# Two changes in a transformer kernel: row-maximum pieces in five of six attention steps, and a 64-row block padded to 128 rows

## The chip, the cores and the metric

The kernel runs on one core of a Trainium2 chip. A core has five engines that run side by side and wait for each other through semaphores: TensorE (PE in the profile: matmuls; PEld its weight loads), VectorE (DVE), ScalarE (ACT), GpSimd (POOL) and SyncE (SP, which issues transfers). Matmul results land in PSUM, eight banks of 512 columns; everything else stands in SBUF. The metric is the device time in microseconds (us) of one execution.

## The reference, cut to what matters

Two transformer layers over 2 x 1024 tokens of 256 features, each layer an attention and a feed-forward part, each followed by a sum with its input and a layer norm. The change touches the second layer alone: its softmax attention (16 heads, 128 plain and 64 rotated query columns, values of 128) and its feed-forward part with integer weights (704 hidden features).

```python
q = (x @ wq).reshape(b, s, H, QH).transpose(0, 2, 1, 3)
...
scores = jnp.einsum('bhqd,bhkd->bhqk', qs, ks_) * scale
scores = jnp.where(causal, scores, jnp.finfo(scores.dtype).min)
attn = jax.nn.softmax(scores, axis=-1)
out = jnp.einsum('bhqk,bhkd->bhqd', attn, v)
...
gate = jax.nn.silu(_qlinear(x, wq_gate, s_gate))
up = _qlinear(x, wq_up, s_up)
return _qlinear(gate * up, wq_down, s_down)
```

Batch and length come from the input, so there are two sequences of 1024 tokens; the attention is causal.

## The kernel before, in words

Float32 products are made from parts of shorter mantissa: a tile `x` is split into `x_hl[0]` (high) and `x_hl[1]` (the rest), and three matmuls (high-high, high-low, low-high) stand for one. So for each such tile ACT copies the high part, and POOL or DVE subtracts it to get the low part.

**Attention** (`phase_attention`, once per sequence, 16 heads). Keys are projected back into a shared space of 128 columns, so all heads use one `k_hl` and one `v_hl`; what is made per head is `q_hl`. Heads go in rounds of four (`rounds`, a hardware loop over rounds with its last one written out). A head has six steps x = 0 to 5, one for each group of two key tiles: groups 0 and 1 serve the first 512 queries, groups 2 to 5 the last 512. Every engine has a function `step(u, r, x, ...)` that lists what it does in that step, in its own program order, and waits for the others by counted semaphores. In step x of head r

- PE makes the scores two groups ahead (`scores`, L1386 products, L1390 mask, L1392 subtraction of the row maximum): in step 0 those of group 2, in steps 4 and 5 those of groups 0 and 1 of the next head. It also makes pieces of the next head's row maxima (`max_piece`, L1370, with L1373 for a piece on the diagonal), query tiles for the next pair of heads (`queries` L1348, `turn` L1362) and the values of group x (`values`, L1406).
- ACT takes the exponential (`probs` L1465), copies the high part (`highs` L1472), copies queries (`row` L1452, `q_high` L1458) and, after groups 1 and 5, the sums (`sums` L1480, L1481).
- POOL subtracts for the low part of the probabilities (`low` L1525) and adds the two halves of the rotation (`rotated` L1519).
- DVE reduces each maximum piece (`peaks` L1578), multiplies for the rotation (`rope` L1561, L1564), makes the queries' low part (`q_low` L1572), and divides the sums of an earlier head (`divide`, L1605 reciprocal and L1607 product). When all pieces of a half are in, `spread` joins them (L1587, or L1590 for the first half) into `whole` and writes `minus` (L1593), a diagonal tile with the negated maxima, which `scores` of the next head need: the first half's in step 4, the second half's (group 2) in step 0 of the next head.

A head's maxima come in twelve pieces, numbered 0 to 11. Row tiles 0 to 3 have one piece (128, 256, 384 and 512 columns wide), row tiles 4 to 7 have two (384 and 256, 512 and 256, 512 and 384, 512 and 512 columns), the second of which lies on the diagonal. The list that sets which piece stands in which step is

```python
PIECES_AT = [(0, 1, 2), (3, 4), (5, 6), (7, 8), (9, 10), (11,)]
```

The first piece of a step stands between the two halves of the scores, a middle one after them, and the last one between the two halves of the values. Two PSUM banks take the pieces in turn, so piece y waits until piece y - 2 is reduced. In heads with even r query tiles are made in all six steps, in heads with odd r only in steps 4 and 5; DVE divides in steps 0 to 3 of heads with even r and in steps 2 to 5 of heads with odd r. In step 1 of odd r DVE also splits new query weights (`weights`).

**Feed-forward part** (`phase_feed_forward`). Tokens go in 4 chunks of 512, hidden features in 6 blocks: five of 128 and a last one of 64 (`HT`). For each chunk and block PE makes gate and up products (`gate_up`, L1889), ACT the activation (L1933) and the high part (L1924), DVE the product of the two (L1973), POOL the low part (L1947). `down_of(t)` (L1902) makes the output of one tile of 128 tokens: 2 parts times 6 blocks, twelve matmuls of 256 columns, of which the two of the last block have 64 rows. The four tiles of a chunk stand between the gate and up products of the next chunk; those of the last chunk stand at the end. The phase begins behind a barrier of all engines.

Of the kernel before, what the change touches and what calls it, by code (L numbers as in the profile page):

```python
# [13 lines left out]
F32 = mybir.dt.float32  # L14
# [8 lines left out]
P = 128  # L23
B, S, C = 2, 1024, 256
# [32 lines left out]
HT = [(n * P, min(P, HID - n * P)) for n in range((HID + P - 1) // P)]  # L57
# [1158 lines left out]
def phase_attention(nc, name, bank, cst, bf, x_hl, wqk_rows, w_raw, w_hl, k_hl, v_hl, oT, last_den):  # L1216
# [10 lines left out]
    with Memory(nc, name) as m:  # L1227
# [38 lines left out]
        AHEAD = 2  # L1266
        HEADS = 4
        ROUNDS = H // HEADS
        PIECES_AT = [(0, 1, 2), (3, 4), (5, 6), (7, 8), (9, 10), (11,)]
        QUARTERS = WIDE // P  # L1270

        def span(group):
# [49 lines left out]
        with nc.Block() as block:  # L1322
# [224 lines left out]
            def _(dve):  # L1547
# [61 lines left out]
                def step(u, r, x, more, peak_pieces, made, turned):  # L1609
                    for y in peak_pieces[:1]:  # L1610
                        peaks(u, r + 1, y)
                    if made:
                        rope(u, *made)
                    for y in peak_pieces[2:]:
                        peaks(u, r + 1, y - 1)
                    if more and x == NG - 1:
                        spread(u, r + 1, 1)
                    if turned:
                        q_low(u, *turned)
                    for y in peak_pieces[1:][-1:]:  # L1620
                        peaks(u, r + 1, y)
                    if more and x == 1:
                        spread(u, r + 1, 0)
                    if r % 2 and x == 1 and not is_round(u, ROUNDS - 1):
                        weights(u, r // 2 + 2)
                    if r % 2 and x >= 2:
                        divide(u, r // 2, 0, x - 2)
                    if r % 2 == 0 and x < QUARTERS and not (is_round(u, 0) and r == 0):
                        divide(u, r // 2 - 1, 1, x)
# [218 lines left out]
def phase_feed_forward(nc, bank, x_hl, x_tok, power, quantised, out):  # L1848
# [4 lines left out]
    NHT = len(HT)  # L1853
    with Memory(nc, "ffn") as m:
# [6 lines left out]
        z = x_tok  # L1861
        norm = LayerNorm(nc, m, z, x_tok, power, 0, NT, 2)
        stored = m.sem("stored")
        gu_mm, gate_sb, hid_sb, hi_sb, lo_sb, y_mm, scaled_sb, z_sb = (
            m.sem(n) for n in ("gu_mm", "gate_sb", "hid_sb", "hi_sb", "lo_sb", "y_mm", "scaled_sb", "z_sb"))
        CT = WIDE // P
# [3 lines left out]
        with nc.Block() as block:  # L1870
            @block.sync
            def _(sp):
                for g in range(norm.groups):
                    sp.wait_ge(norm.x_sb, 2 * (g + 1))
                    at = slice(2 * g, 2 * (g + 1))
                    sp.dma_start(out.rearrange("(t p) c -> p t c", p=P)[:, at, :], x_tok[:, at, :]).then_inc(stored, 16)
                sp.wait_ge(stored, 16 * norm.groups)

            @block.tensor
            def _(pe):  # L1880
                def gate_up(ch, n):
                    h0, hw = HT[n]
                    x = ch * NHT + n
                    if x >= 2:
                        pe.wait_ge(hid_sb, x - 1)
                    for a in range(2):
                        for i in range(2 * KC):
                            part, k = divmod(i, KC)
                            mm = nc.tensor.matmul(bank[0:hw, 2 * (x % 2) + a, :], w[:, a, k, h0:h0 + hw],  # L1889
                                                  x_hl[:, part, k, ch * WIDE:(ch + 1) * WIDE],  # L1890
                                                  start=i == 0, stop=i == 2 * KC - 1)
                    mm.then_inc(gu_mm, 1)

                def down_of(t):
                    ch, i = divmod(t, CT)
                    if t >= 4:
                        pe.wait_ge(z_sb, t - 3)
                    for part in range(2):
                        for n, (h0, hw) in enumerate(HT):
                            if t % CT == 0:  # L1900
                                pe.wait_ge(lo_sb if part else hi_sb, ch * NHT + n + 1)
                            mm = nc.tensor.matmul(bank[:, 4 + t % 4, 0:C], hid_hl[0:hw, part, ch % 2, n, i * P:(i + 1) * P],  # L1902
                                                  down[0:hw, n, :], start=part == 0 and n == 0,
                                                  stop=part == 1 and n == NHT - 1)
                    mm.then_inc(y_mm, 1)

                pe.wait_ge(quantised.w_sb, 4)
                for ch in range(NCH):
                    for n in range(NHT):
                        gate_up(ch, n)  # L1910
                        if ch and 0 <= n - FIRST_DOWN < CT:
                            down_of((ch - 1) * CT + n - FIRST_DOWN)
                for t in range(NT - CT, NT):
                    down_of(t)

            @block.scalar
            def _(act):
                def high(x):
                    n, ch = x % NHT, x // NHT
                    hw = HT[n][1]  # L1920
                    act.wait_ge(hid_sb, x + 1)
                    if n == 0 and ch >= 2:
                        act.wait_ge(y_mm, (ch - 1) * CT)
                    nc.scalar.copy(hid_hl[0:hw, 0, ch % 2, n, :], hid[0:hw, x % 2, :]).then_inc(hi_sb, 1)  # L1924

                act.wait_ge(scales, 16 * (2 * NHT + 1))
                for x in range(NCH * NHT):
                    n = x % NHT
                    hw = HT[n][1]
                    act.wait_ge(gu_mm, x + 1)  # L1930
                    if x >= 2:
                        act.wait_ge(hid_sb, x - 1)
                    nc.scalar.activation(gate[0:hw, x % 2, :], bank[0:hw, 2 * (x % 2), :], ACT.Silu,  # L1933
                                         scale=s_gate[0:hw, n:n + 1]).then_inc(gate_sb, 1)
                    if x:
                        high(x - 1)
                high(NCH * NHT - 1)

            @block.gpsimd
            def _(pool):  # L1940
                for x in range(NCH * NHT):
                    n, ch = x % NHT, x // NHT
                    hw = HT[n][1]
                    if x in norm_at:
                        norm.deviations(pool, norm_at[x])
                    pool.wait_ge(hi_sb, x + 1)
                    nc.gpsimd.tensor_tensor(hid_hl[0:hw, 1, ch % 2, n, :], hid[0:hw, x % 2, :],  # L1947
                                            hid_hl[0:hw, 0, ch % 2, n, :].bitcast(F32), ALU.subtract).then_inc(lo_sb, 1)
                for g in range((NT - CT) // 2 - 1, NT // 2):
                    norm.deviations(pool, g)  # L1950

            @block.vector
            def _(dve):
                def sum_of(t):
                    dve.wait_ge(y_mm, t + 1)
                    nc.vector.tensor_tensor(scaled[:, t % 2, :], bank[:, 4 + t % 4, 0:C], s_down[:],  # L1956
                                            ALU.mult).then_inc(scaled_sb, 1)
                    dve.wait_ge(scaled_sb, t + 1)
                    nc.vector.tensor_tensor(z[:, t, :], scaled[:, t % 2, :], x_tok[:, t, :], ALU.add).then_inc(z_sb, 1)  # L1959
                    if t % 2:  # L1960
                        if t >= 2:
                            norm.normalise(dve, t // 2 - 1)
                        dve.wait_ge(z_sb, t + 1)
                        norm.statistics(dve, t // 2)

                dve.wait_ge(scales, 16 * (2 * NHT + 1))
                for ch in range(NCH):
                    for n, (h0, hw) in enumerate(HT):
                        x = ch * NHT + n
                        dve.wait_ge(gate_sb, x + 1)  # L1970
                        if x >= 2:
                            dve.wait_ge(lo_sb, x - 1)
                        nc.vector.scalar_tensor_tensor(hid[0:hw, x % 2, :], bank[0:hw, 2 * (x % 2) + 1, :],  # L1973
                                                       s_up[0:hw, n:n + 1], gate[0:hw, x % 2, :], ALU.mult,
                                                       ALU.mult).then_inc(hid_sb, 1)
                        if ch and 0 <= n - FIRST_DOWN < CT:
                            sum_of((ch - 1) * CT + n - FIRST_DOWN)
                for t in range(NT - CT, NT):
                    sum_of(t)
                norm.normalise(dve, NT // 2 - 1)  # L1980
# [92 lines left out]
```

## Time and profile before

| | us |
|---|---|
| median of 3 runs | 1520.33 |
| lowest and highest run | 1519.51, 1523.01 |
| the profiled execution | 1521.97 |
| its span, first to last instruction | 1519.4 |
| PE busy | 1295.9 (85%) |
| DVE busy | 966.3 (64%) |
| POOL busy | 821.3 (54%) |
| ACT busy | 653.8 (43%) |

The attention of the two sequences lies at about 500 to 930 and 975 to 1390 us of the span, the feed-forward part from 1429 us on. A row of the timeline has the start, the duration, engine, line, operation, what it writes and reads, shape and count; a bracket at its end is the idle time of its engine just before it and what ended it. A row of the waits says which engine and line waited for which, how long in total, how often, and the longest. A row of the groups by form has the count, the busy time in us, the mean in ns of one, and the idle time before them. A row of the critical chain has the start, the time and the line with its count. Idle time counts where the engine is the one that the others wait for.

### The profile page before, as it was taken

The page shows a single profiled execution, that of the slowest core. Times are in us where ns is not written, and L with a number is a line of the kernel's source. Part 1 is how long each engine was busy: PE and PEld are TensorE (multiplying, and loading weights), DVE is VectorE, ACT ScalarE, POOL GpSimd, SP SyncE. Part 2 cuts the span into 40 slices and gives each one's busy share as a digit, 9 for nine tenths or more (in the row PEclk, how much of TensorE's full clock was granted, in tenths as well). Part 3 has the DMA queues.
Part 4 walks back from the last instruction along what each step waited for, and adds up shares of the span by engine and source line. Part 5 has one row for each costly group of instructions (what it writes and reads, how often), then busy time and mean ns, then how long its engine had stood idle before and what let it go on. Part 6 is the DMA issues. An engine that isn't in the chain of part 4 may idle for free. (4 is left out here: it accounts for less than half of the span.)

```text
span 1519.4 us, 23881 instructions
## 1 busy us (share of the span) xinstructions
PE 1295.9 (85%) x7096; PEld 976.6 (64%) x7097; DVE 966.3 (64%) x2055; ACT 653.8 (43%) x1183; POOL 821.3 (54%) x652
## 2 busy tenths in 40 slices
PE   6965799999944899998999987799999999888797
PEld 5854455555523677776776767677676777767675
DVE  4568422222217778877687768768777877875555
ACT  3211233333212555555555553265555555555332
POOL 2016688888845455545455556354555555556444
PEclk9976799999985999999999999999999999999899
DMA  9357255555552000000000000000000000002001
GB/s 326 121 167 175 86 83 80 80 82 80 80 107 67 8 8 8 1 7 7 1 7 0 2 0 12 15 1 8 8 7 0 7 7 0 1 1 62 1 14 42
DMA packets 66218, 67.13 MB, mean 44 GB/s; under 512 B 15040, under 2 KB 59648, under 8 KB 66016
## 3 DMA queue, kind: packets, MB, share of 16 engines
q1 hardware_dynamic: 48048, 42.38, 9.5%
q0 software_dynamic: 15168, 20.72, 8.8%
q10 hardware_dynamic: 2928, 3.15, 0.7%
q8 instruction: 35, 0.57, 0.2%
q14 instruction: 39, 0.32, 0.1%
HBM read 45.12 MB, written 21.10 MB: 44 GB/s over the span
## 5 line engine op out<-in xcount | busy, mean ns | idle before, releaser
L1525 POOL TENSOR_TENSOR att_prob_lo<-att_prob,att_prob_hi 128x896 fp32r<-128x896 f32 (+1 forms) x192 | 380.4, 1981 | 223.4 <-ACT att_prob_hi L1472 223.4
L1386 PE MATMUL all_bank<-att_q_hl,sequence_k_hl 128*128 128x512 f32 (+2 forms) x1152 | 289.4, 361 | 43.2 <-DVE att_minus L1593 43.0
L1578 DVE TENSOR_REDUCE att_peak<-all_bank 128x1 f32<-128x512 f32 (+3 forms) x384 | 207.8, 550 | 95.0 <-PE all_bank L1373 61.2
L1406 PE MATMUL all_bank<-att_prob_hi,sequence_v_hl 128*128 128x512 f32 (+2 forms) x768 | 225.1, 376 | 12.1 <-ACT late_oT L1481 12.1
L1386 PEld LDWEIGHTS all_bank<-att_q_hl,sequence_k_hl 128*128 128x128 f32 x1152 | 191.6, 192 | 63.9 <-DVE att_minus L1593 33.3
L1465 ACT ACTIVATE att_prob<-all_bank 128x896 f32<-128x896 f32 (+1 forms) x192 | 162.8, 848 | 157.8 <-PE all_bank L1392 156.4
L1370 PE MATMUL all_bank<-sequence_k_hl,att_q_hl 128*128 128x512 f32 (+3 forms) x384 | 164.7, 432 | 6.8 <-DVE att_peak L1578 6.8
L1472 ACT CAST att_prob_hi<-att_prob 128x896 fp32r<-128x896 f32 (+1 forms) x192 | 168.4, 877 | 2.6
L1519 POOL TENSOR_TENSOR att_rows<-att_by_cos,att_by_sin 128x128 f32<-128x128 f32 x128 | 58.5, 457 | 198.6 <-DVE att_by_sin L1564 198.6
L903 PE MATMUL all_bank<-early_w_gu,moe_xgT 128*128 x316 | 147.2, 548 | 3.6 <-issue 2.4
L1406 PEld LDWEIGHTS all_bank<-att_prob_hi,sequence_v_hl 128*128 128x128 f32 x768 | 128.5, 191 | 27.0 <-issue 16.6
L868 POOL DMA_INDIRECT sums<-moe_y,early_slot_far x79 | 125.4, 1587 | 33.9 <-issue 18.9
L1452 ACT COPY att_rows<-all_bank 128x256 f32<-128x256 f32 x128 | 47.5, 371 | 219.9 <-PE all_bank L1348 219.9
L1348 PE MATMUL all_bank<-sequence_w_hl,sequence_x_hl 128*128 128x256 f32 x768 | 125.9, 301 | 15.5 <-DVEq L1633 8.0
L1406 PE MATMUL all_bank<-att_prob_lo,sequence_v_hl 128*128 128x512 f32 (+2 forms) x384 | 133.2, 347 | 0.0
L1392 PE MATMUL all_bank<-att_minus,all_bf 128*128 128x512 bf16 (+2 forms) x384 | 131.5, 342 | 0.0
L1348 PEld LDWEIGHTS all_bank<-sequence_w_hl,sequence_x_hl 128*128 128x128 f32 x768 | 103.6, 197 | 18.0 <-issue 8.8
L995 DVE COPY moe_hidT<-all_bank 112x256 f32<-112x256 f32 x79 | 33.5, 424 | 121.8 <-PE all_bank L913 121.8
L1607 DVE TENSOR_TENSOR late_oT<-late_oT,att_rden 128x128 f32 (+1 forms) x120 | 91.2, 760 | 11.4 <-DVE att_rden L1605 1.6
L858 POOL DMA_INDIRECT moe_xg<-x_rows,early_slot_row x79 | 84.0, 1063 | 26.1 <-issue 21.5
L922 PE MATMUL all_bank<-early_w_down,moe_hidT 112*128 x316 | 86.7, 397 | 13.1 <-issue 11.3
L1370 PEld LDWEIGHTS all_bank<-sequence_k_hl,att_q_hl 128*128 128x128 f32 x384 | 74.3, 194 | 16.7 <-DVE att_peak L1578 8.1
(244 smaller groups left out, 2299.7 us busy)
## 6 DMA issues: line engine op xcount, KB each, us to landing
sequence_w_raw<-wqk_rows SPq DMA_DIRECT2D x16, 256.0 KB, 2.7
early_w_gu<-in_gate SPq DMA_DIRECT2D x16, 224.0 KB, 5.4
early_w_gu<-in_up SPq DMA_DIRECT2D x16, 224.0 KB, 5.5
early_w_down<-in_down SPq DMA_DIRECT2D x1, 3584.0 KB, 20.5
sums<-early_zero SPq DMA_DIRECT2D x18, 128.0 KB, 3.6
all_xT<-in_xT SPq DMA_DIRECT2D x4, 512.0 KB, 8.7
all_x_tok<-in_x SPq DMA_DIRECT2D x1, 2048.0 KB, 17.1
x_rows<-all_x_tok SPq DMA_DIRECT2D x4, 512.0 KB, 3.0
```

Of the source, the lines that this page charges most:

```text
L868: nc.gpsimd.indirect_dma_start(sums[s], bass.IndirectOffsetOnAxis(slot_far[:, r:r + 1], 0), y[:, s, :], None, bounds_check=last_far, compu ...
L903: mm = nc.tensor.matmul(gu_ps[s], xgT[:, s, k, :], w_gu[:, bass.ds(e * (KC * 2 * I) + k * 2 * I, 2 * I)], start=k == 0, stop=k == KC - 1)
L1348: mm = nc.tensor.matmul(q_bank(u, r, t), x_hl[:, xs, k, t * P:(t + 1) * P], w_hl[:, ws, k, :], start=n == 0, stop=n == 3 * KC - 1)
L1370: mm = nc.tensor.matmul(ps[:, 0:w], q_hl[r // 2 % 2][:, 0, r % 2, i * P:(i + 1) * P], k_hl[:, 0, k0:k0 + w], start=True, stop=not diagonal)
L1386: nc.tensor.matmul(ps, k_hl[:, ks, j * P:(j + 1) * P], q_hl[r // 2 % 2][:, qs, r % 2, q0:q0 + w], start=n == 0, stop=False)
L1392: mm = nc.tensor.matmul(ps, bf["ones"], minus[:, r % 2].rearrange("p i m -> p (i m)")[:, q0:q0 + w], start=False, stop=True)
L1406: mm = nc.tensor.matmul(pv_ps[:, q0 - qc * WIDE:WIDE], v_hl[:, vs, j, :], part[:, x % 3, a:z], start=j == 0 and n == 0, stop=last and n == 2)
L1465: nc.scalar.activation(prob[:, x % 2, a:z], s_ps[x % 2][:, a:z], ACT.Exp, scale=SCALE).then_inc(prob_sb, 1)
L1472: nc.scalar.copy(prob_hi[:, x % 3, a:z], prob[:, x % 2, a:z]).then_inc(hi_sb, 1)
L1525: nc.gpsimd.tensor_tensor(prob_lo[:, x % 3, a:z], prob[:, x % 2, a:z], prob_hi[:, x % 3, a:z].bitcast(F32), ALU.subtract).then_inc(lo_sb, 1)
L1578: nc.vector.tensor_reduce(peak[:, r % 2, n, i:i + 1], max_ps[y % 2][:, 0:w], AX_X, ALU.max).then_inc(peak_sb, 1)
L1607: nc.vector.tensor_tensor(own, own, rden[:, n % 2, :], ALU.mult).then_inc(o_sb, 1)
```

## The change

The list of pieces is drawn forward by one piece per step from step 1 on, so that step 5 has none. The second `spread` of a head moves from step 5 to the end of step 4, behind the last maximum. In the feed-forward part the matmuls of the last block use all 128 rows of `hid_hl` and `down`. The 64 rows that nothing else writes are filled with zeros by POOL at the start of the phase, and PE waits for both fills before its first matmul there.

```diff
--- before.py
+++ after.py
@@ -1266,7 +1266,7 @@
         AHEAD = 2
         HEADS = 4
         ROUNDS = H // HEADS
-        PIECES_AT = [(0, 1, 2), (3, 4), (5, 6), (7, 8), (9, 10), (11,)]
+        PIECES_AT = [(0, 1, 2), (3, 4, 5), (6, 7), (8, 9), (10, 11), ()]
         QUARTERS = WIDE // P
 
         def span(group):
@@ -1613,12 +1613,12 @@
                         rope(u, *made)
                     for y in peak_pieces[2:]:
                         peaks(u, r + 1, y - 1)
-                    if more and x == NG - 1:
-                        spread(u, r + 1, 1)
                     if turned:
                         q_low(u, *turned)
                     for y in peak_pieces[1:][-1:]:
                         peaks(u, r + 1, y)
+                    if more and x == NG - 2:
+                        spread(u, r + 1, 1)
                     if more and x == 1:
                         spread(u, r + 1, 0)
                     if r % 2 and x == 1 and not is_round(u, ROUNDS - 1):
@@ -1861,6 +1861,7 @@
         z = x_tok
         norm = LayerNorm(nc, m, z, x_tok, power, 0, NT, 2)
         stored = m.sem("stored")
+        pad_sb = m.sem("pad_sb")
         gu_mm, gate_sb, hid_sb, hi_sb, lo_sb, y_mm, scaled_sb, z_sb = (
             m.sem(n) for n in ("gu_mm", "gate_sb", "hid_sb", "hi_sb", "lo_sb", "y_mm", "scaled_sb", "z_sb"))
         CT = WIDE // P
@@ -1899,12 +1900,13 @@
                         for n, (h0, hw) in enumerate(HT):
                             if t % CT == 0:
                                 pe.wait_ge(lo_sb if part else hi_sb, ch * NHT + n + 1)
-                            mm = nc.tensor.matmul(bank[:, 4 + t % 4, 0:C], hid_hl[0:hw, part, ch % 2, n, i * P:(i + 1) * P],
-                                                  down[0:hw, n, :], start=part == 0 and n == 0,
+                            mm = nc.tensor.matmul(bank[:, 4 + t % 4, 0:C], hid_hl[:, part, ch % 2, n, i * P:(i + 1) * P],
+                                                  down[:, n, :], start=part == 0 and n == 0,
                                                   stop=part == 1 and n == NHT - 1)
                     mm.then_inc(y_mm, 1)
 
                 pe.wait_ge(quantised.w_sb, 4)
+                pe.wait_ge(pad_sb, 2)
                 for ch in range(NCH):
                     for n in range(NHT):
                         gate_up(ch, n)
@@ -1938,6 +1940,9 @@
 
             @block.gpsimd
             def _(pool):
+                last = HT[NHT - 1][1]
+                nc.gpsimd.memset(hid_hl[last:P, :, :, NHT - 1, :].bitcast(F32), 0.0).then_inc(pad_sb, 1)
+                nc.gpsimd.memset(down[last:P, NHT - 1, :].bitcast(F32), 0.0).then_inc(pad_sb, 1)
                 for x in range(NCH * NHT):
                     n, ch = x % NHT, x // NHT
                     hw = HT[n][1]
```

What this does to the order on DVE, at the end of a head with odd r in the loop (steps 4 and 5 up to the first query work of step 5; `att_peak` is a maximum piece, `att_whole` and `att_minus` are the spread, `att_rden` and `late_oT` the division, `by_cos` and `by_sin` the rotation). Before:

```order
L1578 TENSOR_REDUCE att_peak<-all_bank 128x1
L1605 RECIPROCAL att_rden<-att_den 128x128
L1607 ISA
L1607 TENSOR_TENSOR late_oT<-late_oT,att_rden 128x128
L1283 REGISTER_ALU
L1578 TENSOR_REDUCE att_peak<-all_bank 128x1
L1286 REGISTER_ALU
L1561 TENSOR_TENSOR att_by_cos<-att_rows,all_cst 128x128
L1564 TENSOR_TENSOR att_by_sin<-att_rows,all_cst 128x2x32 x2
L1587 TENSOR_TENSOR att_whole<-att_peak 128x4
L1283 REGISTER_ALU
L1593 SCALAR_TENSOR_TENSOR att_minus<-all_bf,att_whole 128x512
```

And of the change, from the same point:

```order
L1578 TENSOR_REDUCE att_peak<-all_bank 128x1
L1587 TENSOR_TENSOR att_whole<-att_peak 128x4
L1283 REGISTER_ALU
L1593 SCALAR_TENSOR_TENSOR att_minus<-all_bf,att_whole 128x512
L1605 RECIPROCAL att_rden<-att_den 128x128
L1607 ISA
L1607 TENSOR_TENSOR late_oT<-late_oT,att_rden 128x128
L1286 REGISTER_ALU
L1561 TENSOR_TENSOR att_by_cos<-att_rows,all_cst 128x128
L1564 TENSOR_TENSOR att_by_sin<-att_rows,all_cst 128x2x32 x2
L1572 TENSOR_TENSOR att_q_hl<-all_bank,att_q_hl 128x2x128
```

The spread now stands ahead of the division of step 4 and of step 5's rotation, and the piece of step 5 is gone.

On PE at the same place, step 4 from the second half of the scores on and the start of step 5 (`att_prob` are values, `att_q_hl,sequence_k_hl` scores, `sequence_k_hl,att_q_hl` of a maximum piece, `att_minus` the end of a half of the scores). Before:

```order
L1386 MATMUL all_bank<-att_q_hl,sequence_k_hl 128x384 x3
L1390 MATMUL all_bank<-all_bf 128x128
L1392 MATMUL all_bank<-att_minus,all_bf 128x384
L1406 MATMUL all_bank<-att_prob_hi,sequence_v_hl 128x512 x2
L1406 MATMUL all_bank<-att_prob_lo,sequence_v_hl 128x512
L1283 REGISTER_ALU
L1370 MATMUL all_bank<-sequence_k_hl,att_q_hl 128x512
L1406 MATMUL all_bank<-att_prob_hi,sequence_v_hl 128x384 x2
L1406 MATMUL all_bank<-att_prob_lo,sequence_v_hl 128x384
L1283 REGISTER_ALU
L1386 MATMUL all_bank<-att_q_hl,sequence_k_hl 128x256 x3
```

And of the change:

```order
L1386 MATMUL all_bank<-att_q_hl,sequence_k_hl 128x384 x3
L1390 MATMUL all_bank<-all_bf 128x128
L1392 MATMUL all_bank<-att_minus,all_bf 128x384
L1406 MATMUL all_bank<-att_prob_hi,sequence_v_hl 128x512 x2
L1406 MATMUL all_bank<-att_prob_lo,sequence_v_hl 128x512
L1283 REGISTER_ALU
L1370 MATMUL all_bank<-sequence_k_hl,att_q_hl 128x512
L1373 MATMUL all_bank<-all_bf 128x128
L1406 MATMUL all_bank<-att_prob_hi,sequence_v_hl 128x384 x2
L1406 MATMUL all_bank<-att_prob_lo,sequence_v_hl 128x384
L1283 REGISTER_ALU
L1386 MATMUL all_bank<-att_q_hl,sequence_k_hl 128x256 x3
```

The piece between the two halves of the values is now one on the diagonal, with a matmul of its mask behind it; the piece that followed in step 5 has moved here.

On POOL at the start of the feed-forward part, of the change (`ffn_hid_hl` the hidden values, `late_w_down` the down weights):

```order
L109 ISA
L1941 UNCONDITIONAL_BRANCH
L1944 MEMSET ffn_hid_hl 64x4x512
L1945 MEMSET late_w_down 64x256
L1952 TENSOR_TENSOR ffn_hid_hl<-ffn_hid,ffn_hid_hl 128x512 x5
L1952 TENSOR_TENSOR ffn_hid_hl<-ffn_hid,ffn_hid_hl 64x512
```

The two fills are new and stand ahead of the first subtraction; the rest is as before.

## Rows read from the trace of the kernel before

**Rows 1.** Waits of PE, both attention phases: line, releaser, us in total, times, longest.

```profile
PE all_bank L1386 <- DVE att_minus L1593: 43.0, 30, 2.8
...
PE all_bank L1370 <- DVE att_peak L1578: 6.8, 12, 0.6
```

**Rows 2.** Timeline of PE over two heads: start us, us, engine line op.

```profile
617.16 0.96 PE L1386 MATMUL all_bank<-att_q_hl,sequence_k_hl 128*128 128x512 f32 x3 [1.79 <-DVE att_minus L1593]
...
618.26 0.23 PE L1373 MATMUL all_bank<-all_bf 128*128 128x128 bf16 x1
618.30 0.96 PE L1348 MATMUL all_bank<-sequence_w_hl,sequence_x_hl 128*128 128x256 f32 x6
...
645.01 0.96 PE L1386 MATMUL all_bank<-att_q_hl,sequence_k_hl 128*128 128x512 f32 x3 [0.91 <-DVE att_minus L1593]
...
669.06 0.96 PE L1386 MATMUL all_bank<-att_q_hl,sequence_k_hl 128*128 128x512 f32 x3 [1.79 <-DVE att_minus L1593]
```

**Rows 3.** Timeline of DVE at the end of the second of these heads.

```profile
663.56 0.69 DVE L1578 TENSOR_REDUCE att_peak<-all_bank 128x1 f32<-128x512 f32 x1 [0.72 <-PE all_bank L1370]
...
665.25 1.60 DVE L1607 TENSOR_TENSOR late_oT<-late_oT,att_rden 128x128 f32 x1
666.78 0.68 DVE L1578 TENSOR_REDUCE att_peak<-all_bank 128x1 f32<-128x512 f32 x1
...
667.85 0.15 DVE L1587 TENSOR_TENSOR att_whole<-att_peak 128x4 f32<-128x4 f32 x1
668.03 0.97 DVE L1593 SCALAR_TENSOR_TENSOR att_minus<-all_bf,att_whole 128x512 bf16<-128x512 bf16 x1
668.92 0.41 DVE L1572 TENSOR_TENSOR att_q_hl<-all_bank,att_q_hl 128x256 fp32r<-128x256 f32 x1
```

**Rows 4.** Timelines of POOL and DVE, the first spread in step 1 of both heads.

```profile
627.48 2.38 POOL L1525 TENSOR_TENSOR att_prob_lo<-att_prob,att_prob_hi 128x1024 fp32r<-128x1024 f32 x1 [0.73 <-ACT att_prob_hi L1472]
...
627.59 2.82 DVE L1593 SCALAR_TENSOR_TENSOR att_minus<-all_bf,att_whole 128x512 bf16<-128x512 bf16 x1
...
652.79 0.69 DVE L1593 SCALAR_TENSOR_TENSOR att_minus<-all_bf,att_whole 128x512 bf16<-128x512 bf16 x1
```

**Rows 5.** Timelines of PE, ACT and POOL in step 4 of the second head.

```profile
663.13 0.39 PE L1370 MATMUL all_bank<-sequence_k_hl,att_q_hl 128*128 128x512 f32 x1
663.36 0.51 PE L1406 MATMUL all_bank<-att_prob_hi,sequence_v_hl 128*128 128x384 f32 x2
...
663.58 0.94 ACT L1472 CAST att_prob_hi<-att_prob 128x896 fp32r<-128x896 f32 x1
...
664.59 2.11 POOL L1525 TENSOR_TENSOR att_prob_lo<-att_prob,att_prob_hi 128x896 fp32r<-128x896 f32 x1 [1.22 <-ACT att_prob_hi L1472]
```

**Rows 6.** Timelines of DVE and POOL in step 4 of the first head.

```profile
640.81 0.68 DVE L1578 TENSOR_REDUCE att_peak<-all_bank 128x1 f32<-128x512 f32 x1
...
641.35 2.10 POOL L1525 TENSOR_TENSOR att_prob_lo<-att_prob,att_prob_hi 128x896 fp32r<-128x896 f32 x1 [1.35 <-ACT att_prob_hi L1472]
```

**Rows 7.** Timeline of PE; windows: busy of PE, PEld, DVE, ACT, POOL, then PEclk.

```profile
720.86 0.96 PE L1386 MATMUL all_bank<-att_q_hl,sequence_k_hl 128*128 128x512 f32 x3 [1.79 <-DVE att_minus L1593]
...
722.05:725.46 3.41, 3.41 (x15) 2.48 (x14) 0.47 (x2) 0.39 (x2) 0.00 (x0) 0.50 0.01 2
```

**Rows 8.** Critical chain of one tile; groups by form; timeline of the output projection.

```profile
1460.81 1.98 PE all_bank L1902 x12
...
L1902 PE MATMUL all_bank<-late_w_down,ffn_hid_hl 64*128 64x256 f32 x32 | 12.2, 381 | 0.2 <-POOL ffn_hid_hl L1947 0.2
...
1394.73 18.20 PE L1711 MATMUL all_bank<-all_vo,out_o_hl 128*128 128x256 f32 x152
```

**Rows 9.** Critical chain: start of the feed-forward part, and its last down products.

```profile
1429.02 3.48 PE all_bank L1889 x8
...
1504.37 6.99 PE all_bank L1902 x37
```

**Rows 10.** Groups by form: a fill on POOL elsewhere in the kernel.

```profile
L648 POOL MEMSET all_xT<- 128x2048 f32 x1 | 1.8, 1804 | 8.3 <-POOLq L110 8.3
```

## The prediction

> **What bounds the kernel now.** I read the waits of TensorE (PE) over both attention phases first. One wait leads: scores wait for the row maxima that VectorE (DVE) spreads into `minus`, 43.0 us in 30 times, and the next one that DVE causes is 6.8 us [rows 1]. The timeline of PE shows where it stands: at every change of head, before the scores of group 2. The head that starts at 617.16 ends in a wait of 0.91 us, the one from 645.01 in one of 1.79 us [rows 2], and this alternates through both phases. I call heads that end in 0.91 even (they also make the next pair's queries) and the others odd; the 30 waits are 16 even and 14 odd ones, and their average, 43.0 / 30 = 1.43 us, lies between. Third, the timeline of DVE at an odd head's end shows why: the last maximum (666.78), `whole` (667.85) and `minus` (668.03, 0.97 us) come at the very end, behind a product of 1.60 us at 665.25 [rows 3]. So in attention PE is the bound, and between heads it hangs on a chain of DVE.
>
> **The lock between DVE and GpSimd.** `minus` takes 0.69 us alone at 652.79, but 2.82 us at 627.59, where GpSimd's subtraction had started 0.11 us before it, at 627.48 for 2.38 us; it ended 0.55 us after GpSimd [rows 4]. So a `minus` that comes just behind a subtraction ends with it + 0.55 us. This decides what the move is worth, since the new place of `minus` is where GpSimd starts the next head's first subtraction. The Trainium skill (SBUF — State Buffer, "Who interferes with whom") says that a DVE instruction with two SBUF inputs contends with a GpSimd instruction that reads SBUF and that the first to start holds the pair for its whole length; the rows above agree, and by the rule too the winner of each race is what counts.
>
> **The move of the maxima.** No instruction is added: twelve pieces, two spreads, as before. One piece goes from step 5 to steps 1 to 4, and the second spread from step 5 to the end of step 4, ahead of the last division of that step.
> - Odd head. PE issues the piece of step 4 between the two value halves at 663.13, and the next matmul follows 0.23 us later [rows 5]. The piece there becomes the diagonal one, whose short matmul takes 0.23 us [rows 2]: its result stands at 663.13 + 0.23 + 0.23 + 0.04 = 663.63. The maximum takes 0.69 us as at 663.56, `whole` to `minus` 0.18 us [rows 3], with 0.04 us between: `minus` starts at about 663.63 + 0.69 + 0.04 + 0.18 = 664.54. ScalarE's copy ends at 663.58 + 0.94, and GpSimd's subtraction starts at 664.59 [rows 5]. Both chains hang on the same PE step, so the lead of 0.05 us stays when the head shifts. I take it that DVE is first: `minus` ends at 665.2, 2 us before PE is ready (669.06 - 1.79 = 667.27), and the 1.79 us go. The bound on the other side: GpSimd first, `minus` ends at 664.59 + 2.11 + 0.55 = 667.25, still in time, but rope and `q_low`, which stand behind it, stay where they are (`q_low` ends at 668.92 + 0.41 = 669.33 [rows 3]), while PE now comes to the queries 618.30 - 617.16 = 1.14 us after its start [rows 2], at 668.4. That is a new wait of 0.9 to 1.0 us, and only 0.8 us of 1.79 are left.
> - Even head. In step 4 DVE is held by `q_low` until its maximum at 640.81, while GpSimd's subtraction starts at 641.35 for 2.10 us [rows 6]. The maximum ends at 641.5, so `whole` and `minus` come after the subtraction's start: they end at 641.35 + 2.10 + about 0.75 = 644.2, and later by some 0.3 us, since in step 2 the wide piece now stands first and makes DVE late. PE is ready at 645.01 - 0.91 = 644.10. I keep 0.46 us of the 0.91, between 0.15 and 0.9.
> - Sum: 43.0 less 14 times 0.46 = 36.6 us (the even head at the end of each sequence makes no queries and has no `q_low` to be held by). The third piece in step 1 I cost at nothing: the spread behind it is held until GpSimd ends at 627.48 + 2.38 anyway [rows 4]. Without that cover it is one maximum of 0.42 us in each even head, 6 us in all.
>
> **The clock.** After the 1.79 us wait at 720.86 TensorE runs a stretch of 3.41 us at 0.50, that is 1.2 instead of 2.4 GHz [rows 7]. Five such stretches start within 2 us of a wait of this kind or of the 2.8 us one near 879; none starts behind a wait of 0.9 us. At most each costs 3.41 / 2 = 1.7 us, 8.5 us in all, and at least nothing comes back. I take 6.
>
> **The padded block.** Twelve down matmuls of one tile take 1.98 us on the critical chain [rows 8]. The 152 matmuls of the same 128x256 shape in the output projection, all with 128 rows, take 18.20 us, 0.120 us each or 1.44 for twelve [rows 8]. The two 64-row ones of a tile are what differs: their mean is 381 ns [rows 8]. With 128 rows I expect the spacing of the others, 0.54 us per tile, 8.6 us over 16 tiles. At the end tile 12 stands before GpSimd's last `lo` (PE goes on at 1504.37 [rows 9]), so what tile 11 and half of tile 12 gain is waited away: 1.5 tiles, 0.8 us. Left 7.8; the bounds are 0 and 8.6.
> The Trainium skill (TensorE: Matmul & The Clock Gate, "Why this matters for your kernels") has a matmul over 32 rows take the same time as one over 128. By that the padding buys nothing; the 381 ns speak against it here, and it is a rival below.
> Against it stand two fills on GpSimd, which PE now waits for. A fill of 2048 columns took 1.80 us [rows 10]; the other, of 256, is 0.23 at that rate. GpSimd and PE leave the same barrier, and PE's first gate matmul starts at 1429.02 [rows 9], so its start moves by about 2.1 us. Nothing hides this, as the first activation hangs on that matmul; at most another 1.7 us of low clock comes with it, at least nothing if GpSimd leaves the barrier early. Net 7.8 - 2.1 = 5.7 us.
>
> **Sum.** 36.6 + 6 + 5.7 = 48.3 us off the profiled execution, whose own time is 1521.97 us (span 1519.4). That is 1.6 us above the median 1520.33. Against the median: 1520.3 - 48.3 = 1472.
>
> **The rivals.**
> - GpSimd wins the race in odd heads. For it: a lead of 0.05 us is less than what a register instruction more could eat. Against it: both chains are rigid. The 14 odd boundaries keep 1.0 us each, and some low clock stays: 14 + 2 less gain, 1488.
> - The waits come back elsewhere on DVE: the 6.8 us for maxima [rows 1] grow, as three pieces stand in step 1 and DVE is late in step 2 and 3. If each head loses 1 us more in this way, 30 us of the attention's gain are lost: about 1502.
> - The padded matmuls take what the 64-row ones take. Then only the fills are left: 7.8 us more, 1480.
> - Slower: the spread in step 4 is locked in every head, and the division behind it too, before rope and `q_low`. The place is the queries in step 0. The price is a lock of 2.1 + 0.55 us, and it decides from a mean of 1.43 + (6 + 5.7) / 30 = 1.8 us of new wait per head. At the full 2.65 us it gives 30 x (2.65 - 1.43) = 37 us more, less 5.7, with no clock back: about 1551. Against it: DVE has waits of its own in step 0 in which it catches up.
>
> **How the numbers follow.** Forecast (DVE first in odd heads) 0.50; GpSimd first 0.24; waits elsewhere 0.12; padding without gain 0.07, on top of either of the first two; slower 0.04; 0.03 for a sum near zero. The forecast's own range is 1462 to 1482: all 8.5 us of clock, 0.9 us in even heads and a free start below, 4 us of clock and 0.15 us in even heads above. The range for 8 in 10 takes in GpSimd first with its own spread: 1461 to 1496. About 0.2%, 3 us, is what a measurement of this kernel can tell from no change: faster 0.93, within 0.03, slower 0.04.
>
> **What would show it.** Right: the wait of scores for `minus` falls from 43.0 us to under 10; in odd heads `minus` starts just before the subtraction and takes 0.69 us; a tile's twelve down matmuls take 1.4 us; the gate matmuls start 2 us later after the barrier. Wrong: a `minus` of 2.6 us in odd heads with queries waiting for `q_low` about 1 us (the first rival); waits for maxima above 20 us (the second); down matmuls still at 1.98 us per tile (the third); queries waiting over 2 us in every head (the last).

## The result, and the profile after

The changed kernel takes 1470.3 us in the median of 4 runs (1462.73 to 1471.49), against 1520.56 (1519.51 to 1523.01) before: a ratio of 0.9656 with an interval of 0.9628 to 0.9683. The forecast was 1472, with a range of 1461 to 1496. The profiled execution took 1471.49 us. The ratios and intervals leave out runs that took more than 1.5% longer than the fastest of the same kernel: one of before (1534.59 us), and one of `later_spread` below, which took 3768.65 us for a cause that stays open.

```profile
span 1469.1 us, 23884 instructions
PE 1278.5 (87%) x7096; PEld 966.7 (66%) x7097; DVE 973.3 (66%) x2055; ACT 655.6 (45%) x1183; POOL 826.6 (56%) x654
```

It is best compared in three parts. The first, from the start to the first head of the attention, is touched by no edit, and yet lay between 503.9 and 517.9 us in the runs of this study. So the other two tell more than the totals. The first head starts where PE makes the scores of group 2 for it. The times are from the PE timeline and the critical chain of each profiled execution.

| us | to the first head | from it to the feed-forward part | feed-forward part |
|---|---|---|---|
| before | 514.3 | 914.6 | 90.5 |
| changed | 515.9 | 870.3 | 82.9 |
| difference | +1.6 | -44.3 | -7.6 |

The waits of PE in both attention phases of the changed kernel answer to [rows 1]; four of them tell the story:

```profile
PE all_bank L1370 <- DVE att_peak L1578: 10.9, 16, 1.6
PE all_bank L1406 <- ACT late_oT L1481: 7.4, 16, 1.1
...
PE all_bank L1348 <- DVE att_q_hl L1572: 6.0, 20, 0.4
PE all_bank L1386 <- DVE att_minus L1593: 5.7, 14, 0.5
```

The last was 43.0 us and the first 6.8 [rows 1]. The other two were, before:

```profile
PE all_bank L1406 <- ACT late_oT L1481: 12.1, 18, 1.1
...
PE all_bank L1348 <- DVE att_q_hl L1572: 5.5, 13, 0.4
```

Together 37.4 us of waiting are gone. The timeline of PE shows where, as [rows 2] did for before:

```profile
590.92 0.96 PE L1386 MATMUL all_bank<-att_q_hl,sequence_k_hl 128*128 128x512 f32 x3 [0.38 <-DVE att_minus L1593]
612.93 0.84 PE L1386 MATMUL all_bank<-att_q_hl,sequence_k_hl 128*128 128x512 f32 x3
...
628.41 0.50 PE L1370 MATMUL all_bank<-sequence_k_hl,att_q_hl 128*128 128x512 f32 x1 [0.66 <-DVE att_peak L1578]
629.31 0.95 PE L1348 MATMUL all_bank<-sequence_w_hl,sequence_x_hl 128*128 128x256 f32 x6 [0.39 <-DVE att_q_hl L1572]
```

The odd head from 590.92 to 612.93 takes 22.0 us, against 669.06 - 645.01 = 24.05 before, and ends in no wait. The even head behind it takes 27.66 us, against 27.85 before [rows 2]. Its wait at the end fell from 0.91 to 0.38 us (at 640.59, where the next odd head begins). Inside it stand waits of 0.66 and 0.39 us; the head of before had two much like them:

```profile
632.11 0.38 PE L1370 MATMUL all_bank<-sequence_k_hl,att_q_hl 128*128 128x256 f32 x1 [0.58 <-DVE att_peak L1578]
633.00 0.95 PE L1348 MATMUL all_bank<-sequence_w_hl,sequence_x_hl 128*128 128x256 f32 x6 [0.44 <-DVE att_q_hl L1572]
```

A wait of 0.17 us for `q_low` at 614.29 is new; waits of 0.16 to 0.25 us stand behind eleven of the odd heads in this way.

The ends of an odd and of an even head on DVE and POOL, which answer to [rows 3, 5] and [rows 6]:

```profile
609.69 0.69 DVE L1578 TENSOR_REDUCE att_peak<-all_bank 128x1 f32<-128x512 f32 x1 [0.79 <-PE all_bank L1373]
610.42 0.16 DVE L1587 TENSOR_TENSOR att_whole<-att_peak 128x4 f32<-128x4 f32 x1
610.62 0.69 DVE L1593 SCALAR_TENSOR_TENSOR att_minus<-all_bf,att_whole 128x512 bf16<-128x512 bf16 x1
...
610.67 2.61 POOL L1525 TENSOR_TENSOR att_prob_lo<-att_prob,att_prob_hi 128x896 fp32r<-128x896 f32 x1 [1.23 <-ACT att_prob_hi L1472]
...
637.13 0.68 DVE L1578 TENSOR_REDUCE att_peak<-all_bank 128x1 f32<-128x512 f32 x1
637.85 1.96 DVE L1587 TENSOR_TENSOR att_whole<-att_peak 128x4 f32<-128x4 f32 x1
639.84 0.69 DVE L1593 SCALAR_TENSOR_TENSOR att_minus<-all_bf,att_whole 128x512 bf16<-128x512 bf16 x1
...
637.68 2.11 POOL L1525 TENSOR_TENSOR att_prob_lo<-att_prob,att_prob_hi 128x896 fp32r<-128x896 f32 x1 [1.33 <-ACT att_prob_hi L1472]
```

In the odd head `minus` is first by 0.05 us, and it is POOL that is held (2.61 us where 2.11 is its own time). In the even head POOL is first by 0.17 us, and the tiny `whole` of 4 columns takes 1.96 us instead of 0.16. No half-clock stretch stands behind a change of head any more; there were five of 3.41 us before [rows 7]. (One stands at the start of the first head, from 514.52 to 517.93 us, where before had none.)

The critical chain at the start of the feed-forward part, where [rows 8, 9] stood:

```profile
1386.19 1.80 POOL ffn_hid_hl L1944
1387.99 0.26 POOL late_w_down L1945
...
1388.39 3.64 PE all_bank L1890 x8
...
1408.31 1.41 PE all_bank L1903 x12
1409.73 1.84 PE all_bank L1890 x8
```

The fills hold PE for 1388.39 - 1386.19 = 2.2 us. A tile's down products take 1.41 us instead of 1.98 [rows 8], and the eight gate products behind them 1.84 instead of 2.04, which the chain showed before:

```profile
1450.77 2.04 PE all_bank L1889 x8
```

### The profile page after: what moved, and what is told of

Its sections match the earlier page's. It is cut to its first block and busy times, and to the rows that moved or that the text cites. A ratio compares the mean times of both kernels' runs of the same rounds, so it can differ in the third digit from the quotient of the medians.

```text
span 1469.1 us, 23884 instructions
## 1 busy us (share of the span) xinstructions
PE 1278.5 (87%) x7096; PEld 966.7 (66%) x7097; DVE 973.3 (66%) x2055; ACT 655.6 (45%) x1183; POOL 826.6 (56%) x654
## 5 line engine op out<-in xcount | busy, mean ns | idle before, releaser
L1386 PE MATMUL all_bank<-att_q_hl,sequence_k_hl 128*128 128x512 f32 (+2 forms) x1152 | 282.5, 354 | 5.8 <-DVE att_minus L1593 5.7
L1406 PE MATMUL all_bank<-att_prob_hi,sequence_v_hl 128*128 128x512 f32 (+2 forms) x768 | 231.1, 384 | 7.5 <-ACT late_oT L1481 7.4
L1370 PE MATMUL all_bank<-sequence_k_hl,att_q_hl 128*128 128x512 f32 (+3 forms) x384 | 168.3, 441 | 11.1 <-DVE att_peak L1578 10.9
L1348 PE MATMUL all_bank<-sequence_w_hl,sequence_x_hl 128*128 128x256 f32 x768 | 121.9, 296 | 16.4 <-DVEq L1633 7.9
L1406 PEld LDWEIGHTS all_bank<-att_prob_hi,sequence_v_hl 128*128 128x128 f32 x768 | 120.3, 193 | 14.6 <-issue 12.0
L1607 DVE TENSOR_TENSOR late_oT<-late_oT,att_rden 128x128 f32 (+1 forms) x120 | 94.3, 786 | 11.4 <-DVE att_rden L1605 1.6
L922 PE MATMUL all_bank<-early_w_down,moe_hidT 112*128 x316 | 87.3, 399 | 12.6 <-issue 10.9
```

The source lines that it names most:

```text
L1348: mm = nc.tensor.matmul(q_bank(u, r, t), x_hl[:, xs, k, t * P:(t + 1) * P], w_hl[:, ws, k, :], start=n == 0, stop=n == 3 * KC - 1)
L1370: mm = nc.tensor.matmul(ps[:, 0:w], q_hl[r // 2 % 2][:, 0, r % 2, i * P:(i + 1) * P], k_hl[:, 0, k0:k0 + w], start=True, stop=not diagonal)
L1386: nc.tensor.matmul(ps, k_hl[:, ks, j * P:(j + 1) * P], q_hl[r // 2 % 2][:, qs, r % 2, q0:q0 + w], start=n == 0, stop=False)
L1406: mm = nc.tensor.matmul(pv_ps[:, q0 - qc * WIDE:WIDE], v_hl[:, vs, j, :], part[:, x % 3, a:z], start=j == 0 and n == 0, stop=last and n == 2)
L1607: nc.vector.tensor_tensor(own, own, rden[:, n % 2, :], ALU.mult).then_inc(o_sb, 1)
```

## The experiments

My theory: the odd heads gain because `minus` beats GpSimd's subtraction in step 4 by a hair; the even heads lose that race and keep some 0.4 us; the padding and the fills are worth what the chain shows, apart from the attention. The rival: it is drawing the pieces forward that matters, and the race decides nothing. Times in the text are medians against a before of 1520.3 to 1521.6 us; windows are the second and third column of the table.

**Each change alone.** `maxima_only` has the new list and the moved spread, `pad_only` only the feed-forward edits.

> The attention part of the change alone, the feed-forward part as before. From the two traces the feed-forward phase, barrier to end, takes 90.5 us before and 82.9 us after, so this kernel is expected 7.6 us above the changed one: 1478 us. The scores' wait for the maxima stays at 5.7 us. Rival: the two parts help each other (a PE that runs without gaps keeps its clock into the feed-forward part); then it is over 1483 us.

> The padded block alone, the attention as before: 1520.5 less 7.6, 1513 us, with the twelve down matmuls of a tile at 1.41 us and the wait of 43.0 us for the maxima unchanged. The rival that padding gains nothing by itself gives 1522.5 us (the fills alone, 2.1 us).

Measured: 1478.6 us (0.9696, 0.9597 to 0.9794) and 1514.1 (0.9937, 0.9896 to 0.9978). The second total is within 2% of before; the windows separate the two cleanly: 868.5 and 90.7 us for the first, 911.7 and 83.0 for the second. Within 3 us the two add up and don't act on each other. The attention of `pad_only` is that of before (42.9 us of waiting for `minus`), and its window is 2.9 us shorter: in that execution half-clock stretches stand behind three changes of head and not five (at 619.7, 879.1 and 1196.5 us, the second twice as long).

**The pieces drawn forward, the spread left in step 5** (`spread_stays`):

```diff
+                    if more and x == NG - 1:
+                        spread(u, r + 1, 1)
                     if turned:
                         q_low(u, *turned)
...
-                    if more and x == NG - 2:
-                        spread(u, r + 1, 1)
```

> The changed kernel with the pieces drawn forward, but the second spread left in step 5 behind the rotation. If what counts is where the spread stands (and which engine holds the port there), an odd head's spread comes behind the locked product of the division and the rotation, about 0.6 us earlier than in the kernel before, one maximum; the wait for the maxima stays above 20 us and the time is about 1498 us. Rival: the freed piece in step 5 is what gives the time; then the wait is under 10 us and the time 1470 to 1476 us.

```profile
PE all_bank L1386 <- DVE att_minus L1593: 39.7, 28, 2.9
```

Measured: 1505.0 us (0.9862, 0.9763 to 0.9961), window 903.9. The total is within 2% of before; again the window tells. The pieces alone take 3.3 us off the wait (39.7 against 43.0 us); 33.6 of the 44.3 us come from the spread's place. The other 10.7 us come with the list. Beside the 3.3 us, the waits on the sums' copy and on `q_low` fell by 4.7 and 2.4 us and those for maxima rose by 2.5. And with gaps at the heads' ends of 1.15 and 1.46 us instead of 0.91 and 1.79, four of the five half-clock stretches went (one is left, at 876.1 us). How the 10.7 us divide between waits and clock stays open.

**Whose turn it is in step 4.** `late_spread` puts a copy of 128 columns on DVE ahead of the second spread in odd heads, `later_spread` a reduction of 384 columns.

```diff
                     if more and x == NG - 2:
+                        if r % 2:
+                            nc.vector.tensor_reduce(spare[:], cst["cos"][:, 0:384], AX_X, ALU.max)
                         spread(u, r + 1, 1)
```

> The changed kernel with one more copy of 128 columns on DVE ahead of the second spread in heads with odd r: some 0.2 us of work, 3 us in all. If the 0.05 us by which the spread starts ahead of GpSimd's subtraction decides, GpSimd now starts first: minus takes about 2.6 us there, queries wait about 0.9 us for the late q_low, and 14 heads lose 0.8 to 1.2 us each: 1482 to 1487 us. Rival: DVE has the slack and the race decides nothing; then 1470 to 1473 us.

Measured: 1467.2 us, window 868.5. The copy fell into the time in which the spread waits for the maximum to end, and `minus` still came 0.04 us ahead of POOL (552.09 against 552.13). It did not move what it was to move, and tells nothing about the race.

> The changed kernel with one more DVE reduction of 384 columns from SBUF (about 0.47 us) between the last maximum and the second spread in heads with odd r; its result is used by nobody. The copy of 128 columns did not move the spread, since it ran in the time in which the spread waits for the maximum's end anyway; this one ends about 0.35 us later than that. If the race with GpSimd decides, GpSimd starts first: whole and minus end 0.6 to 0.75 us behind it, queries wait about 1 us for q_low, and odd heads go from 22.05 to between 22.8 and 23.3 us; the attention of both sequences is 10 to 17 us longer. Rival: DVE has the slack; the odd heads stay within 0.1 us of 22.05.

Measured: 1483.8 us (0.975, 0.9729 to 0.9771), window 892.0, 21.7 more than the change (by the medians, in which the uneven first part lies too, it is 13.5). An odd head's end on DVE, POOL and PE:

```profile
609.50 0.54 DVE L1623 TENSOR_REDUCE att_spare<-all_cst 128x1 f32<-128x384 f32 x1
609.96 2.05 DVE L1588 TENSOR_TENSOR att_whole<-att_peak 128x4 f32<-128x4 f32 x1
612.04 0.69 DVE L1594 SCALAR_TENSOR_TENSOR att_minus<-all_bf,att_whole 128x512 bf16<-128x512 bf16 x1
...
609.87 2.12 POOL L1526 TENSOR_TENSOR att_prob_lo<-att_prob,att_prob_hi 128x896 fp32r<-128x896 f32 x1 [1.22 <-ACT att_prob_hi L1473]
...
612.79 0.96 PE L1387 MATMUL all_bank<-att_q_hl,sequence_k_hl 128*128 128x512 f32 x3 [0.50 <-DVE att_minus L1594]
...
614.78 0.98 PE L1349 MATMUL all_bank<-sequence_w_hl,sequence_x_hl 128*128 128x256 f32 x6 [0.67 <-DVE att_q_hl L1573]
```

`whole` of 4 columns takes 2.05 us and ends with POOL's subtraction, so it is that subtraction, and not the length of the added 0.54 us, that sets when `minus` comes. PE pays 0.50 to 0.60 us for `minus` at twelve odd boundaries and 2.61 us at the last one of each sequence, and the wait for `q_low` behind the boundary shown is 0.67 us instead of 0.17. That is the prediction's first rival, at about its price in these twelve (it said 1.0 us). The window grew by more than the 10 to 17 us that I expected, in part through the two last boundaries. So the race decides, and the rival to the theory falls. But with the race lost, the window is still 22.6 us below the 914.6 of before: by the windows the lead is worth about half of the 44.3 us, and the pieces and the spread's earlier place the other half.

**The first spread ahead of the last maximum of step 1** (`early_first`). In the changed kernel, and in the experiment:

```profile
622.95 0.41 DVE L1578 TENSOR_REDUCE att_peak<-all_bank 128x1 f32<-128x256 f32 x1
623.28 0.15 DVE L1590 COPY att_whole<-att_peak 128x4 f32<-128x4 f32 x1
623.57 2.88 DVE L1593 SCALAR_TENSOR_TENSOR att_minus<-all_bf,att_whole 128x512 bf16<-128x512 bf16 x1
...
623.50 2.40 POOL L1525 TENSOR_TENSOR att_prob_lo<-att_prob,att_prob_hi 128x1024 fp32r<-128x1024 f32 x1 [0.73 <-ACT att_prob_hi L1472]
```

```profile
623.09 0.15 DVE L1590 COPY att_whole<-att_peak 128x4 f32<-128x4 f32 x1
623.37 0.69 DVE L1593 SCALAR_TENSOR_TENSOR att_minus<-all_bf,att_whole 128x512 bf16<-128x512 bf16 x1
623.98 0.42 DVE L1578 TENSOR_REDUCE att_peak<-all_bank 128x1 f32<-128x256 f32 x1
...
623.63 2.69 POOL L1525 TENSOR_TENSOR att_prob_lo<-att_prob,att_prob_hi 128x1024 fp32r<-128x1024 f32 x1 [0.72 <-ACT att_prob_hi L1472]
```

> The changed kernel with the first spread of step 1 ahead of the step's last maximum (it needs pieces 0 to 3 alone). In the trace of the changed kernel even heads take 26.4 us in the first round, where minus starts 0.02 us ahead of GpSimd's subtraction and takes 0.69 us, and 27.65 us in the two rounds of the hardware loop, where it starts 0.07 us behind and takes 2.88. If the race makes that difference, minus now starts 0.3 us ahead in all of them, and the eight even heads of the loop take 26.4 to 26.6 us: 8 to 10 us less in the attention. Rival: the loop's own register instructions make the difference; then they stay at 27.6 us.

Measured: 1455.3 us (0.9566, 0.9547 to 0.9584), window 853.9, 16.4 less than the change. In the changed kernel `minus` loses this race by 0.07 to 0.08 us in seven of the eight even heads of the loop. In the one shown it stays until 626.45, and the maximum of step 2 is late; that is the wait of 0.66 us at 628.41. Ahead of the maximum it wins by 0.26 us, the wait for maxima falls from 10.9 to 3.4 us and that for `q_low` from 6.0 to 1.9, and these heads take 26.25 us instead of 27.65. So the loop's register instructions are not what cost the time. The gain is twice what I had expected: the last even head of each sequence, outside the loop, had lost this race too (by 0.05 us) and takes 20.4 us instead of 21.5, and in three odd heads a wait of 0.44 us for maxima is gone; the rest stays open.

**The fills waited for only before the first down product** (`fills_late`), and both edits (`both_better`):

```diff
                 pe.wait_ge(quantised.w_sb, 4)
-                pe.wait_ge(pad_sb, 2)
...
+                            if ch == 1 and n == FIRST_DOWN:
+                                pe.wait_ge(pad_sb, 2)
                             down_of((ch - 1) * CT + n - FIRST_DOWN)
```

> The changed kernel with PE's wait for the two fills moved to the first down matmul (GpSimd waits for its own fills before its first subtraction). The first gate matmul starts 2.2 us earlier behind the barrier, and the feed-forward phase takes 80.7 instead of 82.9 us. Rival: the first activation's table load or the low clock at the phase's start hides the 2.2 us; then it stays at 82.5 to 83.

> The last two edits together: 10 to 12 us below the changed kernel's 1470, 1458 to 1460 us, by the theory of the race. Without it, 1468.

```profile
1374.53 0.04 issue
1374.57 3.77 PE all_bank L1890 x8
```

Measured: 1460.8 us (0.9619, 0.9588 to 0.965) and 1452.9 (0.9558, 0.9538 to 0.9579). The chain of `fills_late` starts with PE again, and the feed-forward part takes 80.9 and 81.1 us in the two instead of 82.9: the fills' 2 us were on the path. The rest of the first total is not from this edit: in its profiled execution (1457.5 us) the attention has the 870.6 us of the changed kernel, and the part ahead of it is short (503.9 us).

**The last maximum of step 4 drawn up** (`piece_up`, on top of both edits), beside the changed kernel and `both_better` once more on one chip. On PE the piece stands ahead of the first half of the values, on DVE:

```diff
+                    if x == NG - 2:
+                        for y in peak_pieces[1:]:
+                            peaks(u, r + 1, y)
                     if turned:
                         q_low(u, *turned)
...
-                    for y in peak_pieces[1:][-1:]:
-                        peaks(u, r + 1, y)
+                    if x != NG - 2:
+                        for y in peak_pieces[1:][-1:]:
+                            peaks(u, r + 1, y)
```

> The changed kernel itself, beside the two versions below. Its parts in the earlier profile: 870.3 us from the first head to the start of the feed-forward part, 82.9 us from there to the end. Both should return within 1 us. The part before the first head was between 504 and 518 us in the runs so far, though no edit touches it; so the total is expected anywhere between 1460 and 1472.

> The first spread ahead of the last maximum of step 1, and the fills waited for only before the first down product, once more. Theory: the two edits add: 855 us from the first head to the feed-forward part and 81 us from there, 17 us less than the changed kernel. Rival: the 17 us of the first comparison came from the uneven part before the first head; then the difference in these two windows is under 5 us.

> Both edits, and in step 4 PE makes the last maximum piece ahead of the first half of the values, DVE reduces it ahead of the queries' low part, and the second spread stands behind that low part. Theory (in even heads the low part holds the maximum, so GpSimd's subtraction comes first): the piece is there about 0.5 us earlier, the maximum lies in the 0.98 us in which DVE waits, whole and minus start about 0.2 us ahead of the subtraction, and the remaining wait of 0.39 us at the end of even heads goes: 14 x 0.39 = 5.5 us less from the first head to the feed-forward part, about 849.5 us. Rival: the wait at the end of even heads is set by the values or by the subtraction's own length; then GpSimd or PE is late elsewhere by as much and the window stays at 855 us.

Measured: 1472.1, 1452.1 (0.9551, 0.9516 to 0.9585) and 1440.1 us (0.9476, 0.9452 to 0.95); windows 870.3 and 83.2, 854.7 and 80.9, 840.3 and 80.9. The first two return. An even head of the third, DVE and POOL:

```profile
631.05 0.69 DVE L1582 TENSOR_REDUCE att_peak<-all_bank 128x1 f32<-128x512 f32 x1 [0.29 <-PE all_bank L1373]
631.74 0.42 DVE L1576 TENSOR_TENSOR att_q_hl<-all_bank,att_q_hl 128x256 fp32r<-128x256 f32 x1
632.08 0.15 DVE L1591 TENSOR_TENSOR att_whole<-att_peak 128x4 f32<-128x4 f32 x1
632.27 0.70 DVE L1597 SCALAR_TENSOR_TENSOR att_minus<-all_bf,att_whole 128x512 bf16<-128x512 bf16 x1
...
632.62 2.31 POOL L1529 TENSOR_TENSOR att_prob_lo<-att_prob,att_prob_hi 128x896 fp32r<-128x896 f32 x1 [1.32 <-ACT att_prob_hi L1476]
```

`minus` now wins by 0.35 us, no wait of the scores for it is left, and even heads take 25.3 us. 14.4 us are gone instead of the 5.5 expected. The wait for `minus` (5.7 us) and that for `q_low` (0.3 us left of 2.8) account for 8.2. For the rest, PE is busy 5.7 us less in the window (799.2 against 804.9 us) with the same matmuls; the cause stays open. The edit moves a piece on PE as well as two operations on DVE, and no run separates the two. This version beats both kernels.

## Why the prediction was right

- **Odd heads.** The lead of 0.05 us over GpSimd and the vanished wait came as worked out; the waits of 0.16 to 0.25 us for `q_low` behind eleven of them were not forecast. `later_spread` shows what the other outcome of that race costs. The forecast gave DVE's being first a chance of 0.50, so that so small a lead held is in part luck.
- **Even heads.** Forecast 0.46 us of wait kept 14 times, measured 0.38 to 0.48. The mechanism is the one named: `q_low` ahead of the maximum, then GpSimd first, and `minus` ending 0.74 us after GpSimd (637.68 + 2.11 = 639.79, 640.53). `piece_up` takes that order away, and the wait with it.
- **The third piece of step 1, costed at nothing.** In the loop's even heads the cover was there as I said (the spread stays held until 626.45), and the maximum of step 2 is late behind it by 0.61 to 0.66 us, much as it was before (0.58). What I did not see is that the piece moves the race in step 1, and in both directions. In six even heads outside the loop `minus` had lost it by 0.01 us and now wins it by 0.01 to 0.12 us; in four of them a wait of some 0.5 us for maxima and one of some 0.4 us for `q_low` go with it. In the last even head of each sequence it had won by 0.28 us and now loses by 0.05, and PE waits some 0.85 us for a maximum behind it; ahead of it the added piece itself waits 0.74 us. With these, three waits of 0.44 us in odd heads, and two of 2.0 us together in the head at 712.79, the wait for maxima rose by 4.1 us in all: the second rival, in small. The wait for the sums' copy on ACT fell by 4.7 us (from 0.63 to 0.38 us in fourteen odd heads) and paid for it. That was luck; its cause stays open.
- **Clock.** All five stretches are gone, and the window fell by 44.3 us where the waits fell by 37.4, which leaves 6.9 for the clock and whatever else; 6 were forecast. PE was busy 7.4 us less in the window (811.2 against 818.6 us) with the same matmuls. How many of these stretches come varies: three in `pad_only`.
- **Padded block.** Forecast 5.7, measured 7.6 us (7.5 in `pad_only`). A tile's gain is 1.98 - 1.41 = 0.57 us (0.54 forecast), 9.1 us over 16 tiles, and the fills cost 2.2 - 0.1 (2.1 forecast). The term left out is what the 64-row matmuls do to their neighbours: the gate products between the down tiles gain too, up to 0.20 us each time and 1.5 us in all. On the chain, the stretch from the first down tile to the last gate products fell from 51.5 to 43.7 us, of which eleven tiles explain 6.3. The stretch behind it fell from 19.1 to 17.1 us, 0.8 less than its five tiles would give, as forecast. Before the fills the gain is 9.8 us, above the bound of 8.6 that I had set.

The Trainium skill's rule that a matmul over 32 rows takes as long as one over 128 (TensorE: Matmul & The Clock Gate, "Why this matters for your kernels") would have let the padding gain nothing; in this stream, with 64 rows, it gained, as the fall of 1.98 to 1.41 us shows. Whether the 64-row matmul itself takes longer or the change between row counts costs the time, no run separates. The Trainium skill's rule that the first of DVE and GpSimd holds the pair (SBUF — State Buffer, "Who interferes with whom") does hold here: `whole` takes 0.16 us where DVE is first and 1.96 us where GpSimd is.

## What to carry to other kernels

Where two engines race for a shared resource, read who starts first and by how much, for each place where the order can put them; here a lead of a few hundredths of a microsecond stood in for 1 to 2 us, more than twenty times. Put the short operation that others wait for ahead of anything that may delay it, even by one reduction, and take the lead to some tenths. And compare stages, not totals, when a part that no edit touches varies by more than the edit.

## What was not expected

In the profiled executions of the changed kernel and of all runs that keep its order in step 4 (`late_spread` with its copy among them), that race falls out the same way at every odd boundary, though the lead is only 0.04 to 0.06 us. The race in step 1 is less even: in the head at 712.79 the changed kernel won it by 0.03 us, while `late_spread` lost it by 0.30 us in the same head. The loser's price is lopsided: where DVE wins, GpSimd is held by 0.2 to 0.5 us; where GpSimd wins, DVE is held by 1.8 to 2.2 us. And the part ahead of the attention, the same in all kernels, took 503.9 to 517.9 us; the cause stays open.
